# A gated delta net on one core: the gate z projected by tokens, the state decayed on GpSimd, the norm of q moved into the RMS norm

## The reference

```python
q, k, v, z = split(x @ W_qkvz)              # per key head: 128, 128, 2*128, 2*128 columns
q, k, v = silu(causal_conv(q)), silu(causal_conv(k)), silu(causal_conv(v))
q = q * rsqrt(sum(q*q) + 1e-6) / sqrt(128)  # l2 norm, scaled
k = k * rsqrt(sum(k*k) + 1e-6)
# per chunk c, per value head; attn is the inverse of a unit lower triangle (64x64)
v_prime = value_corrected[c] - k_cumdecay[c] @ state
out[c]  = (q[c] @ state) * g_exp[c] + intra[c] @ v_prime
state   = state * g_exp_last[c] + (k[c] * k_decay[c]).T @ v_prime
core    = out * silu(z)
core    = core * rsqrt(mean(core*core) + 1e-6) * norm_weight
y       = core @ W_out
```

## Time and profile before

| | |
|---|---|
| median of 3 runs | 3162.8 us (3155.71 to 3166.08) |
| the profiled execution | 3170.36 us, its span 3168.4 us |
| TensorE matmul busy | 2841.4 us, 90% of the span |
| TensorE weight load busy | 2180.3 us, 69% |
| VectorE busy | 1743.9 us, 55% |
| ScalarE busy | 1548.3 us, 49% |
| GpSimd busy | 361.7 us, 11% |
| mean granted TensorE clock | 0.94 of full speed |

### The profile page before, as it was taken

The page is one execution under the profiler, slowest core; times in us unless marked ns, Lnnn a source line. Parts: engine busy times, 40 slices in busy tenths (PEclk is TensorE's granted clock), DMA queues, the critical chain, the costliest instruction groups (busy, mean ns, idle before and its releaser), DMA issues. The chain is left out here.

```text
span 3168.4 us, 79399 instructions
## 1 busy us (share of the span) xinstructions
PE 2841.4 (90%) x31700; PEld 2180.3 (69%) x31700; DVE 1743.9 (55%) x4255; ACT 1548.3 (49%) x3945; POOL 361.7 (11%) x731
## 2 busy tenths in 40 slices
PE   7899879999659999999999999989999998689998
PEld 4433559999526777677676677767767767579997
DVE  4443556666245556556555555655655555476663
ACT  1123222322136676677667667667666766422221
POOL 0011000000002111111111111111111111000000
PEclk9889889999779999999999999999999999889999
DMA  1000012010000000000000000000000000011100
GB/s 44 25 1 1 26 42 81 27 53 26 5 28 5 12 12 16 5 12 16 5 16 12 16 5 12 15 5 12 15 6 15 12 6 6 26 57 53 50 30 13
DMA packets 58891, 65.34 MB, mean 21 GB/s; under 512 B 16064, under 2 KB 50256, under 8 KB 58576
## 3 DMA queue, kind: packets, MB, share of 16 engines
q1 hardware_dynamic: 58576, 60.92, 6.2%
HBM read 59.86 MB, written 1.05 MB: 19 GB/s over the span
## 5 line engine op out<-in xcount | busy, mean ns | idle before, releaser
L1362 PE MATMUL dn_ps<-xnT,dn_w 128*128 128x512 f32 x768 | 378.9, 619 | 18.7 <-issue 11.5
L433 ACT ACTIVATE g_h<-g_ps,g_b_now 128x512 f32<-128x512 f32 x256 | 174.9, 688 | 338.3 <-PE g_ps L457 332.5
L1446 PE MATMUL dn_ps<-dn_zi,dn_wt 64*64 64x64 f32 x5120 | 262.3, 226 | 50.2 <-DVE dn_zi L1800 50.0
L470 PE MATMUL g_ps<-g_w_high,g_h_low 128*128 128x256 f32 x1024 | 290.3, 283 | 0.0
L470 PE MATMUL g_ps<-g_w_low,g_h_high 128*128 128x256 f32 x1024 | 290.2, 283 | 0.0
L470 PE MATMUL g_ps<-g_w_high,g_h_high 128*128 128x256 f32 x1024 | 290.1, 283 | 0.0
L1446 PEld LDWEIGHTS dn_ps<-dn_zi,dn_wt 64*64 64x64 f32 x5120 | 210.7, 139 | 77.1 <-DVE dn_zi L1800 51.9
L1800 DVE TENSOR_TENSOR dn_zi<-dn_ps,dn_mz 128x128 f32<-128x128 f32 x640 | 159.7, 286 | 186.3 <-PE dn_ps L1436 182.1
L1533 ACT ACTIVATE dn_qs<-dn_ps,dn_cf 64x128 f32<-64x128 f32 x448 | 162.3, 362 | 203.3 <-DVE dn_wv L1810 198.8
L1741 DVE SCALAR_TENSOR_TENSOR dn_cv<-dn_raw,dn_cw,dn_cv 128x1024 f32<-128x1024 f32 x192 | 247.5, 1289 | 2.0
L1810 DVE SCALAR_TENSOR_TENSOR dn_wv<-dn_ps,dn_cf,dn_vt 64x128 f32<-64x128 f32 x448 | 156.6, 349 | 147.8 <-PE dn_ps L1461 142.9
(11 more groups left out here) (267 smaller groups left out, 5980.2 us busy)
## 6 DMA issues: line engine op xcount, KB each, us to landing
g_w<-in_fc_dram SPq DMA_DIRECT2D x32, 1024.0 KB, 6.6
dn_w<-in_W_qkvz_dram SPq DMA_DIRECT2D x16, 768.0 KB, 4.4
dn_wout<-in_W_out_dram SPq DMA_DIRECT2D x16, 256.0 KB, 2.6
f_gate<-in_gateT_dram SPq DMA_DIRECT2D x16, 128.0 KB, 2.2
f_up<-in_upT_dram SPq DMA_DIRECT2D x16, 128.0 KB, 2.4
f_down<-in_downT_dram SPq DMA_DIRECT2D x16, 128.0 KB, 2.4
x_res<-in_x_dram SPq DMA_DIRECT2D x1, 1024.0 KB, 5.0
out_dram<-x_res SPq DMA_DIRECT2D x1, 1024.0 KB, 4.7
```

Of the source, the lines that this page charges most:

```text
L433: nc.scalar.activation(h[:, f % 4], h_b[f % 4], ACT.Gelu, bias=b1_now[u // 2][:, f:f + 1]).then_inc(h_ready, 1)
L470: last = pe.matmul(y_b[q % 2][:, 0:D], hidden[:, f, q * P:(q + 1) * P], weights[:, f, :], start=(f == 0 and n == 0), stop=(f == NF - 1 and ...
L1362: mm = pe.matmul(bA if where == "A" else bC, w[:, k, W_COL[u] * P:(W_COL[u] + 1) * P], m.xnT[:, k, b * T:(b + 1) * T], start=(k == 0), sto ...
L1446: mm = pe.matmul(block_of(bD[s], 1, b, h), wt[s][half(h), 1, b, :], zi[s][half(h), b, :], start=True, stop=True)
```

## The change

- The two z projections (four `proj` steps) take 64 tokens as the stationary operand and 128 weight columns as the moving one, sixteen matmuls a step, the two value heads in the lower and upper 64 output partitions. What ScalarE copies out is by tokens already, and silu works on it in place. The transposes of the gate and ScalarE's scaled copies of them are gone.
- `read_state` is eight matmuls of 64 stationary columns: four for k into bank 0, four for q into bank 1. Rows are then in the same order in both, so VectorE makes `wv` in two instructions and ScalarE `qs` in two. `qs` waits for the q matmuls (`PQ_r`), not for `wv`.
- The state's decay is a multiplication of its own on GpSimd (`kept`), and VectorE adds what `update` brings in one instruction. VectorE waits for `kept_r`, and TensorE for `qs_r` before it overwrites bank 1.
- The norm of q isn't applied; its square goes, times 1e-6, into the RMS norm in place of epsilon (`C_QEPS`).
- The squares are taken for two chunks in one ScalarE instruction, and summed by a `tensor_reduce` on VectorE. The table `ge_swapped` and the matmuls that made it are gone.

The core of the diff (declarations of tiles and semaphores, and the coefficients' copies, are left out):

```diff
-                    for k in range(KD):
-                        mm = pe.matmul(bA if where == "A" else bC, w[:, k, W_COL[u] * P:(W_COL[u] + 1) * P],
-                                       m.xnT[:, k, b * T:(b + 1) * T], start=(k == 0), stop=(k == KD - 1))
+                    to = bA if where == "A" else bC
+                    if u < 4:
+                        for k in range(KD):
+                            mm = pe.matmul(to, w[:, k, W_COL[u] * P:(W_COL[u] + 1) * P],
+                                           m.xnT[:, k, b * T:(b + 1) * T], start=(k == 0), stop=(k == KD - 1))
+                    else:
+                        for n in range(2 * B):
+                            c, b = 2 * (mth - 8) + n // B, n % B
+                            for k in range(KD):
+                                for h in range(GRP):
+                                    mm = pe.matmul(to[half(h), part(n)], m.xnT[:, k, b * T + c * C:b * T + (c + 1) * C],
+                                                   w[:, k, W_COL[4 + h] * P:(W_COL[4 + h] + 1) * P], start=(k == 0), stop=(k == KD - 1))
                     mm.then_inc(s_["pj"], 1)
...
-                    wait(pe, "zt_r", n)
+                    wait(pe, "B_e", n)
                     wait(pe, "oT_r", i * 8 + so_far["turn_out"])
-                    for b in range(B):
-                        pe.transpose(bB[:, part(b)], whole(zs[f], b, c), m.ident[:])
                     for b in range(B):
                         for h in range(GRP):
                             mm = pe.matmul(block_of(bB, 2, b, h), col(cf[f], K_CUM, c, b)[half(h)].broadcast_to([C, C]), eye_of(h),
@@ -1457,10 +1465,12 @@
                         wait(pe, "S_r", stateful(i, j, c))
                         for b in range(B):
                             for h in range(GRP):
-
-                                mm = pe.matmul(bank[0][:, part(2 * b + h)], (k_q, q_k)[h](f, b, c), state[:, b, h, :],
-                                               start=True, stop=True)
+                                mm = pe.matmul(bank[0][half(h), part(b)], qkkq[f][:, b, c, 1], state[:, b, h, :], start=True, stop=True)
                         mm.then_inc(s_["PK_r"], 1)
+                        for b in range(B):
+                            for h in range(GRP):
+                                mm = pe.matmul(bank[1][half(h), part(2 + b)], qkkq[f][:, b, c, 0], state[:, b, h, :], start=True, stop=True)
+                        mm.then_inc(s_["PQ_r"], 1)
...
                     if c < NCH - 1:
                         if c == 0:
                             wait(pe, "y_done", kh * 4)
+                        else:
+                            wait(pe, "qs_r", stateful(i, j, c))
                         for b in range(B):
                             for h in range(GRP):
...
@@ -1540,11 +1549,17 @@
                     wait(act, "pj", kh * 12 + (mth + 1))
                     if mth == 0:
                         wait(act, "cvd", kh * 4)
-                    copy(raw[:, u, b, CONV - 1:] if u < 4 else zr[:, u - 4, b, :], bA if a[1] == "A" else bC).then_inc(s_["ev"], 1)
+                    source = bA if a[1] == "A" else bC
+                    if u < 4:
+                        copy(raw[:, u, b, CONV - 1:], source).then_inc(s_["ev"], 1)
+                    else:
+                        if mth == 8:
+                            wait(act, "oz_r", chunk(i, j, 0) - 8)
+                        n = mth - 8
+                        copy(zt[f][:, 2 * n:2 * n + 2], source.rearrange("p (c b n) -> p c b n", c=2, b=B)).then_inc(s_["ev"], 1)
...
-                        dst, src = (vv, cv[:, 2 + h]) if what[0] == "v" else (zs, zr[:, h])
-                        if what[0] == "v":
-                            wait(act, "cvd", kh * 4 + (3 + h))
-                        else:
+                        if what[0] == "z":
                             wait(act, "ev", kh * 12 + (10 + 2 * h))
-                        slot = h if what[0] == "v" else 1 - h
-                        nc.scalar.activation(dst[f][:, :, :, slot, :].rearrange("p b c n -> p (b c) n"),
-                                             src.rearrange("p b (c n) -> p (b c) n", c=NCH), ACT.Silu).then_inc(s_["sl"], 1)
+                            z_half = zt[f][:, 4 * h:4 * h + 4]
+                            nc.scalar.activation(z_half, z_half, ACT.Silu).then_inc(s_["sl"], 1)
+                            return
+                        wait(act, "cvd", kh * 4 + (3 + h))
...
-
-                    wait(act, "B_e", n + 1)
-                    wait(act, "oz_r", n - 3)
-                    for b in range(B):
-                        last = copy(zt[c % 4][:, b, :], bB[:, part(b)], scale=col(cf[f], C_QNORM, c, b))
-                    last.then_inc(s_["zt_r"], 1)
                 elif name == "gram":
...
@@ -1619,12 +1628,10 @@
                 elif name == "read_state":
                     c, = a
                     if c:
-                        wait(act, "w_r", stateful(i, j, c))
+                        wait(act, "PQ_r", stateful(i, j, c))
                         wait(act, "of_r", chunk(i, j, c))
                         for b in range(B):
-                            for h in range(GRP):
-                                rows = slice((1 - h) * C, (2 - h) * C)
-                                last = copy(qs[rows, b, :], bank[0][rows, part(2 * b + h)], scale=col(cf[f], C_GES, c, b)[rows])
+                            last = copy(qs[:, b, :], bank[1][:, part(2 + b)], scale=col(cf[f], K_GE, c, b))
...
-                        squares(i, j, c - 1)
+                    if c % 2 and c > 1:
+                        squares(i, j, (c - 3) // 2)
...
-                wait(act, "ssq_r", chunk(i, j, c))
-                if c == 0:
-                    wait(act, "ms_r", head(i, j))
-                for b in range(B):
-                    last = nc.scalar.activation(junk[:, b], o[:, c, b, :], ACT.Square, accum_out=ssq[:, B * c + b:B * c + b + 1])
-                last.then_inc(s_["ssq_r"], 1)
+            def squares(i, j, n):
+
+                kh = head(i, j)
+                wait(act, "oz_r", chunk(i, j, 2 * n + 2))
+                wait(act, "ssq_r", kh * 4 + (n - 1))
+                nc.scalar.activation(squared[n % 2][:], o[:, 2 * n:2 * n + 2].rearrange("p c b n -> p (c b) n"),
+                                     ACT.Square).then_inc(s_["sq_r"], 1)
 
             start_counts(act, act_sems)
             act.wait_ge(const_loaded, 16 * CONSTS)
@@ -1695,10 +1700,18 @@
                     wait(pool, "BI_r", n + 1)
                     wait(pool, "Z_r", level(i, j, c, 0) - 9)
                     nc.gpsimd.tensor_tensor(w0[s][:], bi[s][:], over_b(m1t), ALU.mult).then_inc(s_["W0_r"], 1)
+                elif name == "read_state":
+                    c, = a
+                    if 0 < c < NCH - 1:
+                        wait(pool, "S_r", stateful(i, j, c))
+                        last_decay = cf[f][:, K_GL:K_GL + GRP, B * c:B * c + B].rearrange("p h b -> p b h")[:, :, :, None]
+                        nc.gpsimd.tensor_tensor(kept[:], state[:], last_decay.broadcast_to([P, B, GRP, DK]), ALU.mult).then_inc(s_["kept_r"], 1)
                 elif name == "update":
                     c, = a
+                    if c == 0:
+                        wait(pool, "sl", kh * 7 + 7)
                     wait(pool, "of_r", chunk(i, j, c) + 1)
-                    nc.gpsimd.tensor_tensor(o[:, c], o[:, c], zt[c % 4][:], ALU.mult).then_inc(s_["oz_r"], 1)
+                    nc.gpsimd.tensor_tensor(o[:, c], o[:, c], zt[f][:, c], ALU.mult).then_inc(s_["oz_r"], 1)
 
             start_counts(pool, pool_sems)
             nc.gpsimd.memset(raw[:, :, :, 0:CONV - 1], 0.0)
@@ -1723,6 +1736,10 @@
 
...
+            def sum_squares(kh, n):
+                wait(dve, "sq_r", kh * 4 + (n + 1))
+                nc.vector.tensor_reduce(ssq[:, 2 * B * n:2 * B * (n + 1)], squared[n % 2][:], AX_X, ALU.add).then_inc(s_["ssq_r"], 1)
...
                         for b in range(B):
-                            for h in range(GRP):
-                                rows = slice(h * C, (h + 1) * C)
-                                last = nc.vector.scalar_tensor_tensor(out=wv[rows, b, :], in0=bank[0][rows, part(2 * b + h)],
-                                                                      scalar=col(cf[f], K_NGE, c, b)[rows],
-                                                                      in1=vt[c % 4][rows, b, :], op0=ALU.mult, op1=ALU.add)
+                            last = nc.vector.scalar_tensor_tensor(out=wv[:, b, :], in0=bank[0][:, part(b)], scalar=col(cf[f], K_NGE, c, b),
...
-                            nc.vector.tensor_copy(state[:, :, 0, :], pairs(bank[1][:, 0:2 * P]))
-                            nc.vector.tensor_copy(state[:, :, 1, :], pairs(bank[0][:, 0:2 * P])).then_inc(s_["S_r"], 1)
+                            nc.vector.tensor_copy(state[:], added_to_state).then_inc(s_["S_r"], 1)
                         else:
```

(26 more changed lines are left out.)

57 lines of the change are left out of this document (27 added, 30 removed).

## The result

| | before | after |
|---|---|---|
| median of 4 runs each | 3162.99 us (3155.71 to 3166.08) | 3069.11 us (3063.20 to 3080.26) |
| the profiled execution | 3170.36 us, span 3168.4 | 3067.49 us, span 3065.5 |
| ratio, 95% interval | | 0.9699 (0.9672 to 0.9727) |

The change saves 93.9 us, 3.0%. First the page of the changed kernel, its shares of busy time.

What follows compares the result with a forecast made beforehand. TensorE, 92% busy in the delta net, bounds the kernel by its own work and its waits. -1.0 - 4.25 = -5.25 us a head, 16 heads -84, last head -6: 3162.8 - 90 = 3073 us, range 3020 to 3120 (62%).

Steps and rivals of the forecast that it cites:

- Z projections and `read_state`: TensorE matmuls in column halves at 55 ns a pass: each z projection 1.96 us, +0.3 us a head in all; `read_state` 1.08 us, unchanged.
- Column halves don't overlap: Rival: z-projection and `read_state` passes take 0.10 us in place of 0.055, net +5.5 us a head, 3246 us; chance 6%.
- TensorE's own work, -1.0 us a head: TensorE's instructions per head: gate transposes -1.76 us, z projections +0.3, tile-shape switches +0.5, together -1.0 us.
- the shape switches: Two z projections following `gram` now differ from it in tile shape; each switch priced at 0.27 us, +0.5 us a head.
- TensorE's waits, -4.25 us a head: TensorE's idle time: 4.65 us a head of waits for ScalarE gone, +0.4 us at the head's end, net -4.25 us.
- four rows counted as gone: TensorE's waits on late ScalarE work, 28.7, 12.5, 10.1 and 9.2 us, 60.5 in all over 13 heads, 4.65 us a head.
- Nothing off the 38.9 us: TensorE's waits for `dn_zi`, VectorE round trips inside the inversion, 38.9 us before, were taken to stay as they were.
- Who gave the waits back: The waits counted as gone were laid to late ScalarE work; ScalarE was to lose 12.6 us a head.
- `kept` hidden: GpSimd's 1.7 us decay product, 6 times a head, hides before `update` needs it; unhidden, it would cost 10 us a head.
- The last head: No next head fills TensorE's time there; the state's path shortens by 7 chunks x 1.6 us, half taken: -6 us.
- The clock: Rival: shorter passes bring a second half-clock stretch in each head, 3.4 us x 16 = 54 us, 3127 us; chance 7%.

## Why the prediction was right, step by step

The time, 3069 us, is 4 us from the 3073 predicted. The idle time fell about as forecast. That the sum is so near is partly luck: TensorE's work, which I had falling, rose, and the clock, which I had left out, made that good.

- **Z projections and `read_state`.** Predicted 1.96 and 1.08 us from 55 ns a pass, measured 1.90 and 1.02. *Column halves don't overlap* was the rival with the right price: the z projections alone one after another cost 99 us. Which half the next pass is in decides it.
- **TensorE's own work, -1.0 us a head.** This step failed, although the busy time fell by 1.2 us: at full clock the work rose, by 0.6 us. The transposes gave their 1.7 us, the shape switches that I priced at +0.5 us didn't show (the four z projections of the head from 1221 us on take 1.89 to 1.90 us each, 1.89 before), and the output's passes, which I had left out, came to stand alone: +2.6 us a head. The clock, for which I had counted nothing, gave 1.8 us. The row in which L1492 ran beside L1446 was in the trace of before, and I did not read it. The Trainium skill ("TensorEngine Tiling (Array Packing)", Key Properties) on a drain at a change of mode was my reason to add the 0.5 us; no run here isolates such a drain.
- **TensorE's waits, -4.25 us a head.** Measured 9.43 - 4.96 = 4.47. Of the four rows counted as gone, 60.5 us, the turn's, `vp`'s and the bank's are; of the 9.2 us for `wt` 6.0 remain. "Nothing off the 38.9 us" for `zi` was a little too good: they became 43.8. That is the balance of several things, as the experiments show: without the shorter update of the state it is 52.5, and without two of the reductions in the way 40.1. The waits of the output's transposes, which I had not listed, fell from 12.6 us (8.3 for VectorE's scaling, 4.3 for ScalarE) to 2.9.
- **Who gave the waits back.** I gave it all to ScalarE. That fell: ScalarE's load put back costs 41 us, the decay on VectorE 25, the transposes alone 17, `wv` in halves 6 or nothing, the wait for `wv` nothing. Put back one by one they give 89 us, near the 94, but as each shifts the others' waits, I don't read the sum as a proof, and the squares' old form and `read_state`'s were never put back. ScalarE lost 10.5 us a head, where I had 12.6. The mis-sized term is the state's decay: counted as 0 outside the last head, worth 25 us. No run shows which part of the change removed the 38.8 us before the turn and for the bank.
- **`kept` hidden.** No one waits for it, and doubling it costs nothing that can be told from none (+5 us). I had priced it at 1.7 us; it takes 1.05, so GpSimd rose by 116 us rather than 163.
- **The last head.** Predicted -6 us beyond its 5.25. The output matmuls of the last heads, before:

```profile
L1515 PE MATMUL dn_ps<-dn_wout,xn x128: 378/379/634, 2443.7 to 2760.2; 128*128 128x256 f32 x128
```

and after:

```profile
L1527 PE MATMUL dn_ps<-dn_wout,xn x96: 379/379/635, 2477.9 to 2657.5; 128*128 128x256 f32 x96
```

From the last issue of weights to it, 260.6 us became 233.7, -26.9 us. That stretch is as long as 2.3 heads, 13 us by -5.68 each; 14 us remain for the bare end, where I had 6.
- **The clock.** As a rival it was to cost 54 us by more stretches at 0.50. It went the other way, from 12 stretches in 13 heads to 8. The pair of profiles makes more of it than other executions do: the profiled one of before had a mean clock of 0.944, the 29 others beside the experiments had 0.946 on average (0.942 to 0.949).

What stays open: how one idle gap more or less turns into a stretch at half clock. The kernels show only that they go together roughly (idle 6.90 us a head with 6.6 at half clock, 4.96 with 3.7, but also 4.90 with 5.5 where the z halves came in turn), and two go against it (5.39 with 2.6 and 5.56 with 0.8, the norms spread out). Why ScalarE's load costs 41 us when two of its parts tried alone (the wait for `wv`, the gate's copies) cost nothing was not taken apart further; `qs` in four halves was not tried alone.

## What to carry to other kernels

When two matmuls write 64 columns each, alternate the halves from one instruction to the next; the loop's order decides between 62 and 104 ns a pass. On a TensorE that is 92% busy, work added or taken away counts in full only where no round trip lies beside it: here 28 us added cost 17, and 2.7 us a head taken away gave nothing. Read the list of the engine that answers TensorE: 0.4 us ahead of a `zi` on VectorE, which I had priced at nothing, was worth 25 us, under a third of it as waits and the rest with the clock. And look at the clock before you credit a change with busy time: here it gave more than the work did.

## What the runs showed of the hardware

**A GpSimd product holds up VectorE instructions that read SBUF.** Two rows of the changed kernel, of the 16 columns that scale a head's coefficients and of `kept`:

```profile
1149.47 1.04 POOL L1708 TENSOR_TENSOR dn_kept<-dn_state,dn_cf 128x512 f32<-128x512 f32 x1
1149.58 0.97 DVE L1779 TENSOR_TENSOR dn_cf<-dn_beta_rk,dn_recips 128x16 f32<-128x16 f32 x1
```

VectorE's product starts 0.11 us after `kept` and ends 0.04 us after it, where its like takes 0.17 us alone. Groups of VectorE by line, 900 to 2210 us. Before:

```profile
L1741 DVE SCALAR_TENSOR_TENSOR dn_cv<-dn_raw,dn_cw,dn_cv 128x1024 f32<-128x1024 f32 x145 | 187.1, 1290 | 1.6
L1763 DVE TENSOR_TENSOR dn_cf<-dn_beta_rk,dn_recips 128x16 f32<-128x16 f32 x12 | 2.1, 175 | 0.4
```

After, with an instruction that reads PSUM for comparison:

```profile
L1758 DVE SCALAR_TENSOR_TENSOR dn_cv<-dn_raw,dn_cw,dn_cv 128x1024 f32<-128x1024 f32 x153 | 208.1, 1360 | 1.7
L1779 DVE TENSOR_TENSOR dn_cf<-dn_beta_rk,dn_recips 128x16 f32<-128x16 f32 x12 | 10.9, 906 | 0.4
L1864 DVE TENSOR_TENSOR x_res<-x_res,dn_ps 128x512 f32<-128x512 f32 x44 | 30.2, 687 | 64.2 <-PE dn_ps L1527 64.2
```

With `kept` made twice:

```profile
L1760 DVE SCALAR_TENSOR_TENSOR dn_cv<-dn_raw,dn_cw,dn_cv 128x1024 f32<-128x1024 f32 x152 | 223.9, 1473 | 1.7
L1811 DVE TENSOR_TENSOR dn_wt<-dn_ai,dn_m 128x128 f32<-128x128 f32 x94 | 26.9, 326 | 3.7 <-ACT dn_ai L1543 3.7
```

A tap's mean is 1290, 1360 and 1473 ns before, with `kept` once and with `kept` twice. Taken apart by what GpSimd did meanwhile, the changed kernel's 153 taps are 1280 ns long in the 94 cases without a GpSimd instruction beside them and 1914 ns in the 12 beside `kept`; beside other GpSimd products they took 1275 to 1416 ns on average. So `kept` isn't all of it: with the decay on VectorE and no `kept` the mean is 1321. The 16 columns went from 175 to 906 ns, and back to 175 without `kept`. The products for `wt` (L1811), whose inputs are both in SBUF, were 288 ns before and are 326 with `kept` twice. Instructions with one tensor in SBUF grew too: the first tap of a convolution (a plain multiplication, L1738 before and L1755 now) went from 746 to 806 ns, 1009 in the 12 cases beside `kept`, and 747 without it; with `kept` twice, a multiplication of 16 columns by a constant took 905 ns, 174 before. Additions that read PSUM and SBUF kept their length, 688 and 687 ns.

The Trainium skill ("SBUF — State Buffer", SBUF: two separate sides) says that a VectorE operation with two SBUF inputs, or in a mode that uses two ports, and a GpSimd operation that reads SBUF take a shared pair of ports for a whole instruction, and that the other waits. The two rows agree. The rule would have told me to price it: 12 taps by 70 ns and 4 first ones by 60, 1.1 us of VectorE a head.

**Tiles of 64x64 off the diagonal ran beside those on it.** The same eight passes took TensorE 1.3 us a head where their neighbours were on the other diagonal, 3.9 where all were on one: 20 against 61 ns a pass.
